# Linear attention step by step: scores moved to sixteen 32x32 tiles in one piece, V moved by 16 DMAs, the state product in one piece behind K

## The reference, cut to what matters

```python
xn = _layernorm(x)
q, k, v = heads(xn @ Wq.T + bq), heads(xn @ Wk.T + bk), heads(xn @ Wv.T + bv)
q, k = softmax(exp(beta) * q), softmax(exp(beta) * k)      # over the 8 channels of a head
kv = cumsum(einsum('zsD,zsd->zsDd', k, v), axis=1)         # a running 8x8 state per head
kn = cumsum(k, axis=1)
out = einsum('zsD,zsDd->zsd', q, kv) / sum(q * kn)
y = x + (out @ Wo.T + bo) + (fp8(xn) @ Wf.T + bf)
```

## Time and profile before

| what | value |
|---|---|
| median of 3 runs | 1252.97 us (1252.83 to 1252.98) |
| the profiled execution's own time | 1250.03 us |
| its span, first to last instruction | 1248.2 us |
| TensorE busy | 1174.9 us, 94% |
| VectorE busy | 977.9 us, 78% |
| ScalarE busy | 744.9 us, 60% |
| GpSimd busy | 321.6 us, 26% |

### The profile page before, as it was taken

One profiled execution on the slowest core, in us unless ns is written; L12 is line 12 of the kernel. 1 busy time (PEld: TensorE's weight loads), 2 busy tenths in 40 slices (PEclk: granted clock), 3 DMA queues, 4 the chain that ended last, 5 costly groups with the idle time before them and its releaser, 6 DMA issues.

```text
span 1248.2 us, 60447 instructions
## 1 busy us (share of the span) xinstructions
PE 1174.9 (94%) x26082; PEld 679.2 (54%) x26082; DVE 977.9 (78%) x1968; ACT 744.9 (60%) x1177; POOL 321.6 (26%) x590
## 2 busy tenths in 40 slices
PE   1459999999999999999999999999999999999996
PEld 1235555555555555555555555555555555555553
DVE  4567887888788788878878887788788778878873
ACT  0456656665666666566666656666665666566652
POOL 3122222322222232222223232222323232222310
PEclk9689999999999999999999999999999999999999
DMA  9022334334334433433333343343343433333331
GB/s 234 21 59 70 81 90 89 78 80 91 82 82 87 89 80 79 90 86 80 85 89 82 77 90 89 78 84 91 81 79 91 84 83 81 91 82 81 72 73 46
DMA packets 156483, 104.64 MB, mean 84 GB/s; under 512 B 111968, under 2 KB 128480, under 8 KB 156256
## 3 DMA queue, kind: packets, MB, share of 16 engines
q1 hardware_dynamic: 155536, 99.76, 35.7%
q10 hardware_dynamic: 720, 1.31, 0.4%
HBM read 40.20 MB, written 16.78 MB: 46 GB/s over the span
## 4 chain that ended last, share of the span: by engine, by line
PE 92%; issue 3%; DVE 2%; DMA 1%; ACT 1%; POOL 1%; SPq 0%; POOLq 0%; DVEq 0%; ACTq 0%
PE s_ps L900 10%; PE a_ps L917 7%; PE a_ps L1018 6%; PE a_ps L999 6%; PE k_ps L873 5%; PE vo_ps L975 5%; PE vo_ps L873 5%; PE k_ps L877 5%; PE k_ps L875 5%; PE vo_ps L884 4%; PE vo_ps L888 4%; PE vo_ps L886 4%; PE vo_ps L877 4%; PE vo_ps L875 4%; PE q_ps L877 4%; PE q_ps L873 4%
## 5 line engine op out<-in xcount | busy, mean ns | idle before, releaser
L521 ACT ACTIVATE q_heads<-qT,cst 128x512 f32<-128x512 f32 x256 | 163.9, 711 | 88.2 <-DVE qT L769 88.2
L407 POOL TENSOR_TENSOR y_sum<-y,y_magic 128x512 f32<-128x512 f32 x64 | 81.4, 1272 | 433.0 <-DVE y_magic L629 433.0
L506 ACT ACTIVATE w_own<-kT,cst 128x512 f32<-128x512 f32 x128 | 85.5, 715 | 166.7 <-DVE kT L711 166.7
L530 ACT ACTIVATE st_seqs<-st_run,cst 128x576 f32<-128x576 f32 x252 | 181.5, 797 | 0.5 <-DVE st_run L665 0.5
L671 DVE TENSOR_TENSOR att<-s_ps,cst 128x512 f32<-128x512 f32 x256 | 163.8, 682 | 0.4 <-PE s_ps L900 0.4
L400 POOL TENSOR_TENSOR x_split<-xn,x_split 128x512 f16<-128x512 f32 x64 | 74.1, 1158 | 291.6 <-ACT x_split L462 284.3
L900 PE MATMUL s_ps<-q_heads,w_own 64*64 64x128 f32 x4096 | 141.3, 275 | 0.6 <-DVE att L671 0.6
L900 PEld LDWEIGHTS s_ps<-q_heads,w_own 64*64 64x64 f32 x4096 | 110.4, 132 | 54.3 <-issue 54.2
L462 ACT ACTIVATE x_split<-xn 128x512 f16<-128x512 f32 x64 | 40.3, 630 | 126.7 <-DVE xn L618 126.7
L873 PE MATMUL k_ps<-w_hi,xT 128*128 128x512 f16 x256 | 98.9, 386 | 17.0 <-DMA xT<-x_split 12.3
L727 DVE TENSOR_TENSOR vp<-vo_ps,vp 128x512 f32<-128x512 f32 x64 | 44.3, 692 | 86.3 <-PE vo_ps L877 86.3
(11 more groups left out here) (136 smaller groups left out, 2287.8 us busy)
## 6 DMA issues: line engine op xcount, KB each, us to landing
v_groups<-vp SPq DMA_DIRECT2D x512, 36.0 KB, 3.1
x_in<-L_attn_x SPq DMA_DIRECT2D x64, 256.0 KB
x_res<-L_attn_x SPq DMA_DIRECT2D x64, 256.0 KB
out<-o_sb SPq DMA_DIRECT2D x64, 256.0 KB
w_own<-L_attn_Wk SPq DMA_DIRECT2D x1, 1024.0 KB, 13.0
w_own<-L_attn_Wq SPq DMA_DIRECT2D x1, 1024.0 KB, 15.0
w_own<-L_attn_Wv SPq DMA_DIRECT2D x1, 1024.0 KB, 16.5
att<-L_ffn_weight_fp SPq DMA_DIRECT2D x1, 1024.0 KB, 18.1
```

The source lines that it names most:

```text
L506: last = sc.activation(k_pairs[:, i.parity, :, c, :], kT[:, :, :], ACT.Copy, scale=pair_mask[:, c:c + 1])
L521: last = sc.activation(q_heads[:, i.parity, :, j, :], qT[:, i.parity, :, :], ACT.Copy, scale=head_mask[:, j:j + 1])
L530: last = sc.activation(st_seqs[:, i.parity, :, :, b, :].rearrange("p g j w -> p (g j) w"), st_run[:, :, :, :].rearrange("p g j w -> p (g j ...
```

## The change

- **Scores.** `k_pairs` and `pair_mask` go away. `kT` gets two buffers and is the stationary side itself, one sequence at a time: 64 matmuls a step on 32x32 tiles instead of 32 on 64x64 tiles (128 records instead of 64). Sequence b reads rows 32b on; half of the heads (`side` 1) is written to the neighbouring column, so that the 16 tiles write 4 PSUM banks: the two of `s_ps`, `t_ps` and `k_ps`. All of it is one piece, behind the Q projection.
- **V.** The layout of `v_groups` follows: 16 DMAs of 32 partitions instead of 8, in two groups of 8 with `turn_x` between them.
- **State product.** Both halves in one piece right behind K; both `mask_state` move up.
- **VectorE.** The four masks stand together behind the shift of Q; `magic` moves behind `add_state`.
- **ScalarE.** The seed of `k_ps` moves behind that of `q_ps` and waits for the first mask (bank 3). The store of the output and the load of the residual are issued here instead of on SyncE, ahead of `st_seqs`.

```diff
@@ sync
-            def move_v(t):
+            def move_v(t, gp):
...
                 for b in range(SEQS):
-                    for gp in range(GP):
-                        to = SP * gp + b % SP
-                        sp.dma_start(v_groups[TOK * to:TOK * (to + 1), t.parity, to, b // SP],
-                                     vp[TOK * b:TOK * (b + 1), t.parity, HEADS // GP * gp:HEADS // GP * (gp + 1)])\
+                    for side in range(2):
+                        frm, to = SP * gp + b % SP, SP * gp + (b + side) % SP
+                        quads = slice(G // GP // 2 * side, G // GP // 2 * (side + 1))
+                        first = HEADS // GP * gp + HEADS // GP // 2 * side
+                        sp.dma_start(v_groups[TOK * to:TOK * (to + 1), t.parity, frm, b // SP, quads],
+                                     vp[TOK * b:TOK * (b + 1), t.parity, first:first + HEADS // GP // 2])\
...
-                    move_v(i - 1)
+                    move_v(i - 1, 0)
                 if (i + 1).exists():
                     turn_x(i + 1)
+                if (i - 1).exists():
+                    move_v(i - 1, 1)
@@ scalar
-                    if (i + 1).exists():
-                        sc.activation(k_ps[:, :], bias[:, MK, :], ACT.Copy).then_inc(kseed_ready, 1)
...
-                    for c in range(SP):
-                        last = sc.activation(k_pairs[:, i.parity, :, c, :], kT[:, :, :], ACT.Copy,
-                                             scale=pair_mask[:, c:c + 1])
-                    last.then_inc(kpairs_ready, 1)
...
                         sc.activation(q_ps[:, :], bias[:, MQ, :], ACT.Copy).then_inc(qseed_ready, 1)
+                        if i.after(1):
+                            act.wait_ge(att_ready, (i - 1).n * 4 + 1)
+                        sc.activation(k_ps[:, :], bias[:, MK, :], ACT.Copy).then_inc(kseed_ready, 1)
...
+                t = i - 2
+                if t.exists():
+                    act.wait_ge(o_ready, (t + 1).n)
+                    act.dma_start(out_t[t.n], o_sb[:, t.parity, :]).then_inc(stored[t.parity], 16)
+                if i.exists():
+                    act.dma_start(x_res[:, i.parity, :], x_t[i.n]).then_inc(r_loaded[i.parity], 16)
@@ vector
-                    mask_scores(t, 0)
-                    mask_scores(t, 1)
-                    if i.exists():
-                        mask_state(t, 0)
+                if t.exists() and i.exists():
+                    mask_state(t, 0)
+                    mask_state(t, 1)
...
-                if (i + 1).exists():
-                    magic(i + 1)
                 if t.exists():
-                    mask_scores(t, 2)
-                    mask_scores(t, 3)
+                    for c in (3, 2, 0, 1):
+                        mask_scores(t, c)
...
                     add_state(t)
+                if (i + 1).exists():
+                    magic(i + 1)
@@ tensor
+            def scores(t):
...
+                for r in range(G // GP // 2):
+                    for side in range(2):
+                        q = G // GP // 2 * side + r
+                        for gp in range(GP):
+                            g = GP * q + gp
+                            for b in range(SEQS):
+                                rows = slice(TOK * b, TOK * (b + 1))
+                                to = SP * gp + (b + side) % SP
+                                last = mm(score_banks[2 * (b // SP) + side][TOK * to:TOK * (to + 1), P * r:P * (r + 1)],
+                                          kT[rows, t.parity, g, :], q_heads[rows, t.parity, g, :, :],
+                                          start=(r == 0), stop=True, skip_group_check=True)
...
-                    scores(t, 0)
                     if i.exists():
                         state(t, 0)
+                        state(t, 1)
...
-                    pe.wait_ge(att_ready, t.n * 4 + 2)
-                    scores(t, 1)
+                    pe.wait_ge(kT_ready, (t + 1).n)
+                    pe.wait_ge(qheads_ready, (t + 1).n)
                     if i.exists():
-                        state(t, 1)
+                        pe.wait_ge(kshift_ready, (i + 1).n)
+                    if t.after(1):
+                        pe.wait_ge(att_ready, t.n * 4)
+                        pe.wait_ge(al_ready, t.n)
+                    scores(t)
```

More of the change, by code:

```diff
@@ L141, in build @@
         seq_mask = cst[:, C_SEQ:C_SEQ + SEQS]
-        pair_mask = cst[:, C_PAIR:C_PAIR + SP]
         tri = cst[:, C_TRI:C_TRI + TOK]
@@ L193, in build @@
         qT = sb("qT", [P, 2, G, TOK])
-        kT = sb("kT", [P, G, TOK])
-        k_pairs = w_own[1][:, :, :].rearrange("p (n c) (g s) -> p n (c g) s", n=2, s=TOK)\
-            .rearrange("p n (g c) s -> p n g c s", c=SP)
+        kT = sb("kT", [P, 2, G, TOK])
         q_heads = sb("q_heads", [P, 2, G, J, TOK])
@@ L221, in build @@
         a_ps = ps("a_ps", 2 * DM)
+        score_banks = [s_ps[:, 0:DM], s_ps[:, DM:2 * DM], t_ps[:, :], k_ps[:, :]]
         a_halves = a_ps[:, :].rearrange("p (n w) -> p n w", n=2)
@@ L668, in mask_scores @@
             def mask_scores(t, c):
-                dve.wait_ge(scores_done, t.n * 2 + c // 2 + 1)
-                v.tensor_tensor(att[:, c % 2, 4 * (c // 2):4 * (c // 2) + 4, :, :]
+                dve.wait_ge(scores_done, (t + 1).n)
+                v.tensor_tensor(att[:, c // 2, 4 * (c % 2):4 * (c % 2) + 4, :, :]
                                 .rearrange("p g j s -> p (g j) s"),
-                                s_ps[:, DM * (c % 2):DM * (c % 2 + 1)].rearrange("p (h s) -> p h s", s=TOK),
+                                score_banks[c].rearrange("p (h s) -> p h s", s=TOK),
                                 tri[:, None, :].to_broadcast([P, 4 * J, TOK]), ALU.mult)\
@@ L704, in key_sums @@
                     for b in range(SEQS):
-                        dve.wait_ge(v_moved[i.parity][b], i.half * 16 * GP)
+                        dve.wait_ge(v_moved[i.parity][b], i.half * 16 * GP * 2)
                 v.reciprocal(vp[:, i.parity, :, DH].rearrange("p (l q j) -> p q l j", l=GP, j=J),
@@ L708, in key_sums @@
                     .then_inc(krec_ready, 1)
-                if i.after(1):
-                    dve.wait_ge(kpairs_ready, i.n)
-                v.transpose(kT[:, :, :].rearrange("p g s -> p (g s)"), k_e[:, i.parity, :])\
+                if i.after(2):
+                    dve.wait_ge(scores_done, (i - 1).n)
+                v.transpose(kT[:, i.parity].rearrange("p g s -> p (g s)"), k_e[:, i.parity, :])\
                     .then_inc(kT_ready, 1)
@@ L769, in body @@
                     v.transpose(qT[:, i.parity].rearrange("p g s -> p (g s)"), q_e[:, :]).then_inc(qT_ready, 1)
-                if t.exists() and i.exists():
-                    mask_state(t, 1)
                 if fold:
@@ L890, in project_out @@
                 return last
-            def scores(t, half):
+            def scores(t):
                 pe.sem_inc(pe_waited, 1)
[L895 to L902, removed]
+                for r in range(G // GP // 2):
[9 more added lines that the diff above has]
+                                          start=(r == 0), stop=True, skip_group_check=True)
                 last.then_inc(scores_done, 1)
@@ L927, in body @@
                 if t.exists():
-                    pe.wait_ge(kpairs_ready, (t + 1).n)
-                    pe.wait_ge(qheads_ready, (t + 1).n)
-                    if t.after(1):
-                        pe.wait_ge(att_ready, t.n * 4)
-                    scores(t, 0)
                     if i.exists():
                         state(t, 0)
+                        state(t, 1)
                 t = i - 2
@@ L1010, in body @@
                     for b in range(SEQS):
-                        pe.wait_ge(v_moved[t.parity][b], (t + 2).half * 16 * GP)
+                        pe.wait_ge(v_moved[t.parity][b], (t + 2).half * 16 * GP * 2)
                     pe.sem_inc(pe_waited, 1)
```

15 lines of the change are left out of this document (3 added, 12 removed).

## The result

The changed kernel takes 1400.21 us (median of 4 runs, 1390.74 to 1413.51), the kernel before 1252.9: a ratio of 1.1164, 95% interval 1.114 to 1.1188. The forecast was 1245.4, with 1268 as its upper end. It was wrong by 155 us, and in sign.

What follows compares the result with a forecast made beforehand. TensorE (94% busy) was the bound; after the change VectorE mostly: even step 17.36 plus odd 18.60 make 35.96 us against 36.30, -10.5 over 31 pairs. 1252.97 - 10.5 + 3 for late landings = 1245.4 us, range 1216 to 1268.

Steps and rivals of the forecast that it cites:

- TensorE alone would then need 17.0 to 17.3 us a step: TensorE's step with two score pieces of 1.03 replaced by one of 1.03 to 1.28, and state pieces joined.
- joined they save one change of shape, about 0.1: TensorE's two state pieces in one run keep their records and save about 0.1 us a step.
- what is free: ScalarE's two DMA issues, about 0.6 each, delay nothing; SyncE's loop with 16 V DMAs fits, 16.0 of 17.98 us.
- `magic`'s late place: GpSimd gets magic behind add_state, so root runs late: a new wait of 2.1 us in every second step.
- the bound that the prediction named: VectorE's chain to o_sb sets the step; TensorE idles before V, 0.1 to 0.4 us and about 1.
- wait for rstd: Line 618 on VectorE waits some 2.1 us every second step; xn starts 3.47 into the odd step.
- first rival: Square root in time, or magic's late place costs nothing: odd step 17.11, -57 us, 1196 us; chance 0.10.
- V lands late: Rival: line 1018 waits for V behind 16 issues on SyncE, +0.22 us a step, +14, 1267 us; chance 0.17.
- only eight tiles run together: Score piece on TensorE: 2.06 us, costing 0 to 0.1 a step; bad case of four, 4.1 us, 1365 us, chance 0.06.
- even step: Step without the late square root, K to next K: 17.36 us, set by VectorE's chain to o_sb.

Runs made afterwards that it cites:

- b_joined: Kernel before with both state pieces and both mask_state behind the first score piece, same number of TensorE records: 1275.36 us, 1.0211.
- a_magic_sp: Changed kernel with output store and residual load issued by SyncE again and magic back ahead of the four masks: 1325.07 us, 1.0598.
- b_act_out: Kernel before with only the output's store and the residual's load issued by ScalarE ahead of st_seqs: 1250.95 us, 0.9993.
- a_sp_out: Changed kernel with the output's store and the residual's load issued by SyncE again: 1333.3 us, 1.0666.
- b_v16_act: Kernel before with V in 16 DMAs around turn_x, and output store and residual load on ScalarE: 1297.73 us, 1.0372.
- a_xq_early: Changed kernel with the transposing DMA of xq issued ahead of V's second DMA group, store and load still on ScalarE: 1474.92 us, 1.1796.
- b_v16: Kernel before with each V DMA cut in two (16 of 18 KB) and turn_x between the two groups: 1261.44 us, 1.0089.
- a_spread: a_magic_sp with the second state piece moved behind the rounded branch and its mask behind qT: 1337.57 us, 1.069.
- a_order: a_magic_sp with the score matmuls ordered by sequence outermost, then side and half: 1323.97 us, 1.0582.

## Why the prediction was wrong

**The step that failed** is "TensorE alone would then need 17.0 to 17.3 us a step". It priced a short matmul by the distance to the next in the earlier trace rows, and so took for granted that its instructions are there. That held for the kernel before, with its 96 short records in a run and 128 on line 1018, all between long matmuls. With 128 in one piece behind K and 128 more in the score piece it doesn't hold: b_joined gives +25 us with not one instruction more. In a_magic_sp, where the crossing is gone, the matmuls of the state and the scores show 17.6 and 29.6 us of waits by issue, where the kernel before has 0.0 and none by issue. "joined they save one change of shape, about 0.1" was the same mistake. How many short records may stand together was not measured.

**The second failed step** is "what is free". The two issues on ScalarE were weighed for ScalarE's time (0.6 each, and indeed free: b_act_out 0.9993) and SyncE's queue for its issue time (16.0 of 17.98), but what the transfers do to each other was not. Moving the transfers to ScalarE costs 64 us (a_sp_out), because V's eight more DMAs push the transposing DMA of xq to the moment at which ScalarE's transfers start. What is paid at the end depends on what is under way then: `quantise`, which writes `xq_rows` (14 waits in b_v16_act, 20 in the changed kernel), V (23 in a_xq_early), or TensorE's own instructions (12 late packets, 40 us of waits, in the changed kernel).

**A third term was missing, a smaller one.** The score piece now writes `t_ps`, from which VectorE makes `al`, so it has to wait for `al`; the prediction laid out when `al` comes and never held it against this piece. That wait is 16.6 us in the changed kernel and 12.2 in a_sp_out, which has no crossing. In a_magic_sp it is 1.7: it is by this way, and not by `o_sb`, that `magic`'s late place reaches TensorE. On the other side, the bound that the prediction named is not there: TensorE was to stand before V until `o_sb` is written, 0.1 to 0.4 us and about 1 a step, and stands there for 1.0 us in the whole run.

**The account.** From the forecast's 1245 to 1397 are 152 us. 64 belong to the crossing, with the late instructions and the lower clock behind its stalls. The other 88 lie between the forecast and a_sp_out, which both have `magic` in its late place. Of these, 49 stand in its trace as waits by issue in front of the state and score matmuls (19.5 + 29.5), if all of them are on the path, and 12 as the wait for `al`. The last 27 I can't divide: the longer score piece (below) would make up to 0.57 x 62 = 35 if it were wholly on the path, and the clock is 0.973 there, not 0.982. No run tested either alone.

**Right, by rows.** The wait for rstd is what was worked out: after the K of 741.64 (the row below is VectorE's timeline) xn starts 3.61 into the odd step, forecast 3.47.

```profile
745.25 0.55 DVE L613 TENSOR_SCALAR xn<-x_in,mv,rstd 128x512 f32<-128x512 f32 x1 [1.55 <-POOL rstd L386]
```

It comes 26 times in the run, 45.6 us in all, where 2.1 in each of 31 pairs would be 65. Its price was wrong: by the first rival's sum it is 49 us (1245 less 1196), and a_magic_sp, which takes it away, gains 8, since other waits cover it. That 16 V DMAs are in time was right for SyncE's queue alone (b_v16), so the rival "V lands late" fell in its own form: the place was SyncE's queue, as it said, but the price was set by another queue. VectorE did not become the bound: 73% busy, not over 80%.

**The score piece.** Between the rivals:

```profile
600.50 0.30 PE L894 MATMUL s_ps<-q_heads,kT 32*32 32x128 f32 x2
...
602.35 1.04 PE L971 MATMUL vo_ps<-w_hi,xq 128*128 128x512 f16 x4
```

An undisturbed piece takes 1.85 (600.50 to 602.35); forecast 1.03 to 1.28, and 2.06 if only eight tiles run together, 4.1 for four. So it is close to eight. By the rule of the Trainium skill, "TensorEngine Tiling (Array Packing)", Restrictions and Gotchas, that different row tiles can't access one PSUM bank at the same time, four tiles would run together and the piece take 4.1, as the prediction worked out; the measurement says no.

**Even a step without a stall misses its mark.** The shortest even step in the middle of the run starts at 762.24 and takes 17.68, where 17.36 was worked out.

## What to carry to other kernels

On TensorE a run of short matmuls has two prices, the array's time and the supply of their instructions. Don't join such runs to save a gap (b_joined), and don't expect that any other place for half of one helps (a_spread); fewer matmuls with more columns each need fewer instructions. Before DMA issues move to another engine's queue, look up what the old queue has in flight at that point of the step: a free issue can delay transfers of a queue that never waits for it, the instructions of TensorE among them. When two parts cost little each (0 and 12 us here), run them together before you call the sum small (46).

## What the runs showed of the hardware that was not expected

- TensorE can run out of instructions in an unrolled program without branches. It goes on about 1.4 us behind a 16 KB packet of the instruction queue, in 55 of 60 waits of the changed kernel, 43 of 44 of a_sp_out and 16 of 16 of b_joined. Single waits on line 911 are up to 4.4 us long.
- Crossing transfers can delay these packets too: one took 4.96 us in the changed kernel, and twelve over 2 us; none over 2 in a_sp_out and, with another order of SyncE's queue, in a_xq_early, two in a_magic_sp (the longest 3.25).
- A transposing DMA that meets two transfers of 256 KB from another engine's queue lands up to 11.4 us after its issue (median 3.9), 4.3 at most without them; V's small DMAs, of 18 KB, up to 9.7 (7.3 without them), and one issue on SyncE took 5.7 (2.1 at most in a_sp_out). Why the queues hold each other up so long was not settled: it may be the engines that they share or the order of the packets.
- 128 fp32 records in sixteen 32x32 tiles over four banks take 1.85 us, about as if eight ran together (an estimate from 1.03 us for 32 records in four tiles), whatever their order (1.84 in a_order).
